# Attention output split in the attention pass by ScalarE and GpSimd, kept in DRAM as two parts, with the loop over batches written out

## What is computed

```python
# x1 = x + attn(layernorm(x)); heads = 8, head dimension 64
qk = x @ W_qk + b_qk; v = x @ W_v + b_v
attn = softmax(q @ k^T / sqrt(64))
o = attn @ v
x1 = x + (layernorm(o @ W_out + b_out) * gamma + beta + xn) / sqrt(2)   # xn = layernorm(x)
# out = x1 + mix(layernorm(x1)); x_prev is the row before
r = sigmoid(mix(x, x_prev, mu_r) @ W_r^T)
k = square(relu(mix(x, x_prev, mu_k) @ W_k^T))
out = x1 + r * (k @ W_v2^T)
```

## Time and profile before

| | |
|---|---|
| median of 3 runs | 2773.16 us (2770.03 to 2774.45) |
| the profiled execution | 2776.32 us |
| its span, first to last instruction | 2774.5 us, mean granted PE clock 0.988 |
| PE | 2641.1 us busy (95%) |
| PEld (weight loads beside PE) | 1784.3 us (64%) |
| DVE | 1685.7 us (61%) |
| ACT | 1295.2 us (47%) |
| POOL | 1422.0 us (51%) |
| attention pass | from 0 to about 1972 us |
| second pass | from about 1973 us to the end |

### The profile page before, as it was taken

The page is one execution under the profiler, slowest core; times in us unless marked ns, Lnnn a source line. Parts: engine busy times, 40 slices in busy tenths (PEclk is TensorE's granted clock), DMA queues, the critical chain, the costliest instruction groups (busy, mean ns, idle before and its releaser), DMA issues. The chain is left out here.

```text
span 2774.5 us, 36018 instructions
## 1 busy us (share of the span) xinstructions
PE 2641.1 (95%) x11376; PEld 1784.3 (64%) x11376; DVE 1685.7 (61%) x2691; ACT 1295.2 (47%) x1789; POOL 1422.0 (51%) x755
## 2 busy tenths in 40 slices
PE   5999999999999999999999999999589999999999
PEld 4655656665565665666566556655367777777777
DVE  5555455555545544654554555454488888888885
ACT  2345245434534533453453354344365555555554
POOL 2475466557647655664674566567323332332333
PEclk9999999999999999999999999999799999999999
DMA  3111021121112112111111211122211111212110
GB/s 106 54 39 43 24 74 43 31 65 36 43 27 66 43 35 62 43 35 50 51 40 31 62 47 31 31 47 61 87 58 65 68 68 65 71 63 73 60 61 31
DMA packets 89739, 145.06 MB, mean 52 GB/s; under 512 B 20096, under 2 KB 20608, under 8 KB 89600
## 3 DMA queue, kind: packets, MB, share of 16 engines
q1 hardware_dynamic: 89600, 143.19, 18.0%
HBM read 75.24 MB, written 33.81 MB: 39 GB/s over the span
## 5 line engine op out<-in xcount | busy, mean ns | idle before, releaser
L403 DVE TENSOR_REDUCE half_max<-ps_max 128x1 f32<-128x512 f32 x1024 | 680.1, 687 | 552.9 <-PE ps_max L743 545.3
L314 POOL TENSOR_TENSOR acc<-acc,probs 128x1024 f32<-128x1024 f32 x384 | 913.7, 2379 | 148.2 <-ACT probs L593 119.8
L593 ACT ACTIVATE probs<-ps_st 128x1024 f32<-128x1024 f32 x512 | 521.7, 1023 | 600.6 <-PE ps_st L764 576.1
L775 PE MATMUL ps_o<-probs,v 128*64 128x512 f32 x2048 | 471.1, 602 | 14.3 <-issue 14.3
L310 POOL TENSOR_TENSOR acc<-probs 128x1024 f32<-128x1024 f32 x64 | 153.2, 2394 | 619.3 <-ACT probs L593 619.3
L763 PE MATMUL ps_st<-qA,kA 128*128 128x512 f32 x1024 | 414.9, 405 | 14.6 <-DMA qB<-max_row 9.4
L764 PE MATMUL ps_st<-qB,kB 65*128 65x512 f32 x1024 | 407.6, 398 | 0.0
L743 PE MATMUL ps_max<-kA,qA 128*128 128x512 f32 x1024 | 387.2, 417 | 10.9 <-DVE half_max L403 4.4
L775 PEld LDWEIGHTS ps_o<-probs,v 128*64 128x64 f32 x2048 | 136.7, 137 | 282.5 <-issue 257.7
L743 PEld LDWEIGHTS ps_max<-kA,qA 128*128 128x128 f32 x1024 | 189.1, 189 | 145.6 <-issue 69.3
L763 PEld LDWEIGHTS ps_st<-qA,kA 128*128 128x128 f32 x1024 | 194.5, 190 | 83.2 <-ACT probs L593 33.7
(11 more groups left out here) (172 smaller groups left out, 4481.3 us busy)
## 6 DMA issues: line engine op xcount, KB each, us to landing
stage<-in_L_attn_x_dram SPq DMA_DIRECT2D x32, 512.0 KB, 6.0
qA<-qA SPq DMA_DIRECT2D x128, 128.0 KB, 2.2
kB<-kA SPq DMA_DIRECT2D x128, 128.0 KB, 2.3
o_scratch<-oT SPq DMA_DIRECT2D x128, 128.0 KB, 2.3
stage<-o_scratch SPq DMA_DIRECT2D x16, 1024.0 KB, 5.6
xc<-in_L_attn_x_dram SPq DMA_DIRECT2D x16, 1024.0 KB, 5.3
out_dram<-gate SPq DMA_DIRECT2D x64, 256.0 KB, 2.0
inv_cols<-inv_scratch SPq DMA_DIRECT2D x126, 128.0 KB, 2.8
```

The lines of the kernel that those rows point to most:

```text
L314: pool.tensor_tensor(acc[:, :], acc[:, :], probs[:, j, :], ALU.add).then_inc(acc_done, 1)
L403: dve.tensor_reduce(half_max[:, r, kh:kh + 1], ps_max[(j + 1) % 2][:, :], AX_X, ALU.max).then_inc(max_done, 1)
L593: act.activation(probs[:, j, :], ps_st[j % 2][:, :], ACT.Exp).then_inc(exp_done, 1)
L775: ins = pe.matmul(ps_o[half * DH:(half + 1) * DH, :], v[:, j, hd * DH:(hd + 1) * DH], probs[:, j, half * HALF:(half + 1) * HALF], start=(j ...
```

## The change

ACT and POOL now split the normalised o in the attention pass: `store_o_hi` on ACT rounds it to fp32r into `oT_hi` (two slices of a tile that is free in this pass), `split_o` on POOL subtracts this from it in place. SP stores both parts, in four transfers instead of two, to two DRAM tensors. The second pass loads both parts of a chunk straight into `o_hi` and `o_lo` and its `split_o` functions are gone, on ACT and on DVE. With them goes the early fetch of the first chunk: it is now loaded first thing in the second pass, and the raw W_out takes its place in `stage[:, 0]`. The loop over batches is replaced by a Python loop on all five engines, so its code stands seven times and its waits compare with constants. The loop of the second pass stays.

```diff
@@ SyncE, attention pass
-                sp.dma_start(w_out_raw[:, :, :], w_out.rearrange("(k p) n -> p k n", p=P)).then_inc(pass2_in, 16)
...
                 def store_o(b, h):
-                    sp.wait_ge(o_done, 8 * b + h + 1)
+                    sp.wait_ge(oT_lo_done, 8 * b + h + 1)
                     for half in range(2):
-                        sp.dma_start(o_scratch[b][half, h, :, :],
-                                     oT[h % 2][half * DH:(half + 1) * DH, :]).then_inc(oT_free[h % 2], 16)
+                        dims = slice(half * DH, (half + 1) * DH)
+                        sp.dma_start(o_hi_scratch[b][half, h, :, :], oT_hi[h % 2][dims, :]).then_inc(oT_free[h % 2], 16)
+                        sp.dma_start(o_lo_scratch[b][half, h, :, :], oT[h % 2][dims, :]).then_inc(oT_free[h % 2], 16)
...
-                        for i in range(2):
-                            sp.wait_ge(oT_free[i], 16 + 128)
-                        sp.dma_start(stage[:, 0], chunks_of(o_scratch)[0]).then_inc(pass2_in, 16)
+                        sp.dma_start(stage[:, 0], w_out.rearrange("(k p) n -> p k n", p=P)).then_inc(pass2_in, 16)
...
-                with sp.Fori(0, B - 1) as b:
+                for b in range(B - 1):
@@ GpSimd (head: the new call stands right behind normalise_o)
+                def split_o(b, h):
+
+                    pool.wait_ge(oT_hi_done, 8 * b + h + 1)
+                    pool.tensor_tensor(oT[h % 2][:, :].bitcast(F32R), oT[h % 2][:, :], oT_hi[h % 2], ALU.subtract).then_inc(oT_lo_done, 1)
...
                     if h >= 2:
                         normalise_o(b, h - 2)
+                        split_o(b, h - 2)
@@ ScalarE (in each kind of head the new call stands right behind store_o)
+                def store_o_hi(b, h, done=o_done):
+
+                    act.wait_ge(done, 1 if done is o_last else 8 * b + h + 1)
+                    act.activation(oT_hi[h % 2].bitcast(F32R), oT[h % 2][:, :], ACT.Copy).then_inc(oT_hi_done, 1)
...
                         store_o(b, h - 1)
+                    if h >= 2:
+                        store_o_hi(b, h - 2)
...
+                store_o_hi(B - 1, HEADS - 2)
+                store_o_hi(B - 1, HEADS - 1, o_last)
@@ second pass, SyncE
                 def load_o(g):
-                    sp.dma_start(o_raw[:, :, :], o_view[g]).then_inc(o_in, 16)
+                    sp.dma_start(f32(o_hi[:, :, :]), o_hi_view[g]).then_inc(o_in, 16)
+                    sp.dma_start(f32(o_lo[:, :, :]), o_lo_view[g]).then_inc(o_in, 16)
...
+                load_o(0)
                 for dst, src in ((bo, b_out), (gam, gamma), (bet, beta)):
...
-                        sp.wait_ge(o_lo_done, g + 1)
+                        sp.wait_ge(y_done, 4 * g + 4)
                         load_o(g + 1)
@@ second pass, VectorE and ScalarE
-                def split_o(g):
-                    dve.wait_ge(o_hi_done, g + 1)
-                    dve.tensor_tensor(o_lo[:, :, :], o_raw[:, :, :], f32(o_hi[:, :, :]), ALU.subtract).then_inc(o_lo_done, 1)
...
-                    act.activation(o_hi[:, :, :], o_raw[:, :, :], ACT.Copy).then_inc(o_hi_done, 1)
@@ second pass, TensorE
-                        pe.wait_ge(o_hi_done, g + 1)
-                        pe.wait_ge(o_lo_done, g + 1)
+                        pe.wait_ge(o_in, 32 * g + 32)
```

More of the change, by code:

```diff
@@ L51, in rows_of, with attention_pass @@
     return 4 + (j - 8) // 2, j % 2
-def attention_pass(nc, x, w_qk, b_qk, w_v, b_v, w_out, w_r, w_out_raw, stage, o_scratch, inv_scratch, ln1_stats, ident):
+def attention_pass(nc, x, w_qk, b_qk, w_v, b_v, w_out, w_r, spare, stage, o_hi_scratch, o_lo_scratch, inv_scratch, ln1_stats,
+                   ident):
     with ExitStack() as ctx:
@@ L89, in attention_pass @@
         oT = [sb(f"oT{i}", [P, HALF]) for i in range(2)]
+        oT_hi = [spare[:, i, :] for i in range(2)]
         xb = stage[:, :, :, :].rearrange("p a k n -> p (a k) n")
@@ L274, in _ @@
                 store_o(B - 1, HEADS - 2)
[L275 to L279, removed]
+                store_o(B - 1, HEADS - 1)
+                sp.wait_ge(pass2_in, 32)
                 for i in range(2):
-                    sp.wait_ge(oT_free[i], 16 + 128 * B)
+                    sp.wait_ge(oT_free[i], 16 + 256 * B)
             @block.gpsimd
@@ L343, in _ @@
                 head(0, 1, False)
-                with pool.Fori(0, B - 1) as b:
+                for b in range(B - 1):
                     for h in range(2, HEADS + 2):
@@ L523, in _ @@
                 head(0, 1, False)
-                with dve.Fori(0, B - 1) as b:
+                for b in range(B - 1):
                     for h in range(2, HEADS + 2):
@@ L548, in keep_stats @@
                     act.wait_ge(rstd_done, b + 1)
[L549 to L550 removed]
+                    act.activation(ln1_stats[:, slice(b * TT, b * TT + TT), 0], mean_var[:, :, 0], ACT.Copy)
+                    act.activation(ln1_stats[:, slice(b * TT, b * TT + TT), 1], rstd[:, :], ACT.Copy).then_inc(stats_kept, 1)
                 def normalise(b, t):
@@ L683, in _ @@
                 head(0, 1, False)
-                with act.Fori(0, B - 1) as b:
+                for b in range(B - 1):
                     for h in range(2, HEADS + 2):
@@ L998, in _ @@
                 head(0, 1, False)
-                with pe.Fori(0, B - 1) as b:
+                for b in range(B - 1):
                     for h in range(2, HEADS + 2):
@@ L1003, in _, with mix_pass @@
                     head(B - 1, h, True)
-def mix_pass(nc, x, o_scratch, w_out_raw, stage, b_out, gamma, beta, w_k, w_v, mu_r, mu_k, out, ln1_stats, ident):
+def mix_pass(nc, x, o_hi_scratch, o_lo_scratch, spare, stage, b_out, gamma, beta, w_k, w_v, mu_r, mu_k, out, ln1_stats, ident):
     with ExitStack() as ctx:
@@ L1036, in mix_pass @@
         y = sb("y", [P, NT, C])
-        x2 = [sb("x2", [P, NT, C]), w_out_raw]
+        x2 = [sb("x2", [P, NT, C]), spare]
         bn6 = sb("bn6b", [P, NT, 6])
@@ L1051, in mix_pass @@
         gate = sb("gate", [P, NT, C])
-        raw = {"out": x2[1][:, :, :], "r": mixed[:, :, :], "k": x2[0][:, :, :], "v": gate[:, :, :]}
+        raw = {"out": stage[:, 0], "r": mixed[:, :, :], "k": x2[0][:, :, :], "v": gate[:, :, :]}
         bank = [ctx.enter_context(nc.psum_tensor(f"bank{i}", [P, C], F32)) for i in range(8)]
@@ L1347, in weight_hi @@
                     act.activation(hi[n][:, kc, :], weight_bank(u), ACT.Copy).then_inc(w_hi_done, 1)
-                def split_o(g):
-                    if not (isinstance(g, int) and g == 0):
-                        act.wait_ge(o_in, 16 * g)
-                    act.activation(o_hi[:, :, :], o_raw[:, :, :], ACT.Copy).then_inc(o_hi_done, 1)
                 def mix_before(g, n, kc):
@@ L1384, in step @@
                             act.activation(sq[:, d % 2, :], relu[:, d % 2, :], ACT.Square).then_inc(sq_done, 1)
-                    if first and not (isinstance(g, int) and g == CHUNKS - 1):
-                        act.wait_ge(y_done, 4 * g + 4)
-                        split_o(g + 1)
                     if second:
@@ L1499, in seq_preln_block @@
         stage = ctx.enter_context(nc.sbuf_tensor("stage", [P, 2, KC, C], F32))
-        w_out_raw = ctx.enter_context(nc.sbuf_tensor("w_out_raw", [P, KC, C], F32))
-        o_scratch = nc.dram_tensor("o_scratch", [B, 2, HEADS, DH, HALF], F32, kind="Internal").ap()
+        spare = ctx.enter_context(nc.sbuf_tensor("spare", [P, KC, C], F32))
+        o_hi_scratch = nc.dram_tensor("o_hi_scratch", [B, 2, HEADS, DH, HALF], F32, kind="Internal").ap()
+        o_lo_scratch = nc.dram_tensor("o_lo_scratch", [B, 2, HEADS, DH, HALF], F32, kind="Internal").ap()
         inv_scratch = nc.dram_tensor("inv_scratch", [2, 2, HALF], F32, kind="Internal").ap()
-        attention_pass(nc, x, w_qk, b_qk, w_v, b_v, w_out, w_r, w_out_raw, stage, o_scratch, inv_scratch, ln1_stats, ident)
-        mix_pass(nc, x, o_scratch, w_out_raw, stage, b_out, gamma, beta, w_k, w_v2, mu_r, mu_k, out, ln1_stats, ident)
+        attention_pass(nc, x, w_qk, b_qk, w_v, b_v, w_out, w_r, spare, stage, o_hi_scratch, o_lo_scratch, inv_scratch, ln1_stats,
+                   ident)
+        mix_pass(nc, x, o_hi_scratch, o_lo_scratch, spare, stage, b_out, gamma, beta, w_k, w_v2, mu_r, mu_k, out, ln1_stats, ident)
 _INS = ["L0_attn_x", "L0_attn_W_qk", "L0_attn_b_qk", "L0_attn_W_v", "L0_attn_b_v", "L0_attn_W_out", "L0_attn_b_out",
```

25 lines of the change are left out of this document (13 added, 12 removed).

## The result

Median 2730.34 us (4 runs, 2730.17 to 2731.35) against 2773.80 us for the kernel before on the same chip (4 runs, 2770.03 to 2775.39): ratio 0.9846, 95% interval 0.9829 to 0.9863. The forecast was 2742 us, with a range from 2734 to 2760. The change gains 43 us where the sum said 31. The sign was right, the size was not.

What follows compares the result with a forecast made beforehand. PE, busy for 95% of the span, was taken as the bound. Terms -18.1 + 1.0 + 3.2 + 1.2 - 18.2 = -30.9 us took the profiled 2776.3 to 2745.4 us, a median of 2742, range 2734 to 2760.

Steps and rivals of the forecast that it cites:

- The written-out loop: Attention pass: removing six jumps back, in heads taking 173.95 us together, saves 18.1 us; register work costs PE nothing.
- Rival B: Written-out code brings its own instruction stalls, as much lost as saved: 2760 us; chance 0.07.
- Turning heads: Attention heads where ACT goes on from o to the turned tiles: its rounding has thin cover, +1.0 us over seven.
- GpSimd's subtraction and SP's stores in the plain heads: Attention pass: POOL's subtraction fits its idle 7.61 us, and four stores leave the query copy about 2.5 us: cost nothing.
- Rival C: Attention pass: rounding, subtraction and four stores delay the copies PE's ninth product needs; 4 us longer gives 2811 us; chance 0.05.
- The change of passes: Between passes: +3.2 us for rounding, subtraction and two more transfers at the end, +1.2 for waiting on two 1 MB loads.
- The steps of the second pass: Earlier `gated` and `store_y` on DVE shorten PE's waits: 1.1 us odd step, 1.4 even, 18.2 for seven pairs.
- Rival A: Second pass: the mixing gains nothing, `gated` of tile 1 moves by 0.1 us only, 1.4 us for 18.2: 2759 us; chance 0.10.
- ACT's rounding in this pass: Second pass: the rounding isn't among PE's waits, so its going is worth nothing.
- The start: From the program's start to the first turned maximum: forecast difference 0.
- low end: Start of the second pass at its lower bound (-2.7), all step waits gone (another 1.2), runs' spread 2 to 4 us: 2734.

Runs made afterwards that it cites:

- the loop alone: Kernel before with only its loop over batches written out on all five engines: 2752.32 us against 2771.43, ratio 0.9933.
- the repeat: Changed kernel run once more, nothing edited: 2731.81 us against 2771.87 for the kernel before, ratio 0.9854.
- held addition: Changed kernel with POOL's addition to tile 0 in the second pass held until DVE's first mixing instruction is done: 2754.34 us, ratio 0.9935 to the kernel before.
- the full instruction on DVE: Changed kernel with a 128x2048 subtraction put back on DVE at its old second-pass place, on an unread tile: 2755.62 us against 2772.82 before, ratio 0.9944.
- half of it: Changed kernel with a 128x1024 subtraction put back on DVE in the second pass: 2736.94 us, ratio 0.9875 to the kernel before.
- the two halves: Kernel before with only the batch loop written out, 2752.32 us (-19.1); changed kernel with the five loops kept, 2747.38 us (-24.0).

## Why the prediction was right and wrong

**The written-out loop: right.** -18.1 was booked, -17.8 us measured on the six heads (156.16 against 173.95), and -19.1 us for the loop alone, with the turning heads in it. But 3.4 us of the term were the lower clock in two heads and not PE's wait. The forecast took all of it for the jump's price; the sum came out because the low clock went from these heads together with the jumps. Rival B (stalls of the written-out code) is next to nothing: four heads are 0.2 to 0.35 us over 25.99, 1.1 us together, and in the same places in the repeat.

**Turning heads: wrong in sign, small.** "So 0.3 us at most come through, nothing at least": +1.0 was booked, -1.8 us came (7 x 0.26). The experiments part the two: ACT's rounding costs nothing there, and the written-out code gives it. Reading that the register work "costs PE nothing" from one plain head didn't hold for heads with a wait in them.

**GpSimd's subtraction and SP's stores in the plain heads: right**, 0 booked and 0 measured. Rival C had no part (its chain of "4.6 us" adds up to 4.5).

**The change of passes: right**, +4.2 us for +4.4: +3.2 for +3.2 at the end of the pass, and 8.06 against 7.13 us, +0.9 for +1.2, at the start of the next. That it fits to 0.2 us is luck in part. Five more profiles of the written-out kernel with the same start of the second pass have their first product 45.6 to 46.3 us behind the last turned maximum, and with the loop alone written out it is 40.88 us in place of 41.79, so that the split's own price is 5.1 us by the written-out kernels and 4.7 by those with the loop (46.46 - 41.79).

**The steps of the second pass: the mechanism was right, the size wrong.** The failed step is: "That clears the first wait. `store_y` ... moves with it, and clears what is left of the second wait (...). So PE gains the smaller of the two". It booked 18.2 us for the 14 steps, and they gave 27.9. Two things in it are off.

First, the wait that the profile lists is not what a wait costs. PE in the kernel before, around one:

```profile
2211.36 0.39 PE L1431 MATMUL bank<-mix_wv_lo,act_hi 128*128 128x512 f32 x1
2211.59 0.39 PE L1431 MATMUL bank<-mix_wv_hi,act_hi 128*128 128x512 f32 x1
2212.91 0.50 PE L1431 MATMUL bank<-mix_wv_hi,act_lo 128*128 128x512 f32 x1 [0.93 <-DVE gate L1245]
2213.25 0.40 PE L1431 MATMUL bank<-mix_wv_lo,act_hi 128*128 128x512 f32 x1
```

In a full stream the starts are 0.227 us apart. Here they are 1.32 and 0.34 us apart: 1.66 - 0.45 = 1.21 us lost, 0.93 listed. The rest is 0.16 us between the start distance and the 0.39 us shown for the last matmul, whose end is modelled, and 0.11 us until the next ones follow closely. So each of these waits costs some 0.27 us more than is listed, and a stop below 0.16 us leaves no gap between the matmuls at all. In the kernel before a pair of steps has five such places, the two of each step and one for ACT's `gate` in the even one:

```profile
PE bank L1431 <- ACT gate L1392: 0.9, 6, 0.2
```

Listed are (11.1 + 7.4 + 0.9) / 7 = 2.8 us a pair, with 5 x 0.27 that is 4.1; measured is 95.01 - 91.10 = 3.9. The held addition agrees: 1.04 us a step listed, two places, 1.58 by this count, 1.64 measured; so does the full instruction on DVE (1.44 listed, 1.98 counted, 2.04 measured). With half of it nothing is listed and 0.54 us is lost: 0.36 at `gated`'s place, 0.14 at `store_y`'s, by the starts. Start distances alone tell that.

Second, DVE gained more than 1.1 us before `store_y`. In the kernel before one of the four mk_lo instructions stands beside POOL's addition of tile 1 and the four take 3.58 us, as in the run with the addition held:

```profile
2260.30 3.58 DVE L1257 TENSOR_TENSOR mk_lo<-stage,mk_hi 128x512 fp32r<-128x512 f32 x4
```

In the kernel after they take 2.49 us, and POOL's two additions 5.19: the same collision, and now GpSimd waits. That gives `store_y` another 1.1 us, of which 0.46 are lost again in the mixing of r (4.22 us in place of 3.76). Nobody waits for that addition, so the step ends with no wait of PE at all. Why the one or the other engine gets its turn isn't settled: in both kernels DVE's first mk_lo starts 0.16 us before the addition. Only that it went the other way is shown.

Rival A (the mixing gains nothing) is what the held addition makes of the kernel: 24 us, where the forecast priced it at 17, for the same two reasons. ACT's rounding in this pass was booked at nothing; putting it back costs some 0.1 us a step.

**The start.** Of -1.8 us up to the first turned maximum the cause stays open; W_out's load isn't it. Without it the profiles differ by 43.1 us; the medians say 43.5, the repeat 40.1, the two halves 43.2.

**The range.** Its low end took the waits listed for PE as the most that could be won. It was bounded by a display and not by the distance between starts.

## What to carry to other kernels

Price a short wait of PE by the distance between the starts of the instructions around it, against the distance in a full stream; with the waits below a microsecond of this kernel the listed idle time understates the loss by a fifth or more, and a loss of a third of a microsecond wasn't listed. Where GpSimd works beside VectorE, look at when its instructions run before moving VectorE's: a freed 2.3 us a step was worth 25 us because it let one addition end before a dense group began, and with that addition held back 0.35 us a step were left of it. Where a wait goes, look at the granted clock of its stretch too: part of its price may be the clock. And load what the first product needs ahead of the rest.

## What the runs showed of the hardware

- A DVE instruction with two SBUF inputs beside a GpSimd one: one of four waits the other out, 1.79 us for 0.75 (mixing) and 1.78 for 0.68 (mk_lo), or GpSimd waits, 3.49 us for 1.29. The Trainium skill (SBUF — State Buffer, Who interferes with whom) has a DVE instruction with two SBUF inputs and a GpSimd one that reads SBUF contend for a port pair that only one of them can hold; the traces agree, in both directions.
- A restart of PE in a stream of 128x512 products costs about 0.27 us beyond the idle time listed, with listed waits from 0.15 to 0.93 us.
- A jump back in the attention loop costs 2.1 to 4.4 us for PE; in the two dearest of the six 1.7 us each are a granted clock of 0.94 in place of 1.00. The 14 steps of the second pass's loop, which also jumps back six times, all take 45.4 to 45.6 us in the changed kernel: no jump shows there, and why is open.
- Loads in pieces: the first 256 KB lands after 2.8 us, the next 256 KB after 3.2, and 1 MB after 5.5 us (median of 15).
